# Two graph layers and two attention layers on one core: where the weights of the first attention layer are split, where two stores are waited for, and the order of the q and k blocks

## The reference

```
x = x + (adj @ h) @ W0 + b0
x = x + (norm_adj @ (h @ W1)) + b1               # norm_adj: adj scaled by its rows' degree
x = x + o + layernorm(o)*gamma + beta,  o = attention(h @ w_qkv, masked where adj == 0) @ w_proj + b_proj
x = x + attention(h@Wq+bq, h@Wk+bk, h@Wv+bv, additive mask (1-adj)*-1e9) @ Wo + bo     # 8 heads of 32
```

## Time and profile before

| | |
|---|---|
| median of 3 runs | 2866.49 us (2864.7 to 2868.12) |
| the profiled execution: time, span | 2864.98 us, 2862.8 us |
| span until the graph phase's last matmul | 478.0 us |
| first score matmul of the attention phase | 506.55 us |
| PE busy over the span | 2809.5 us (98%) |
| DVE, ACT, POOL busy | 2319.6, 2175.3, 590.0 us |

### The profile page before, as it was taken

One profiled execution on the slowest core, in us unless ns is written; L12 is line 12 of the kernel. 1 busy time (PEld: TensorE's weight loads), 2 busy tenths in 40 slices (PEclk: granted clock), 3 DMA queues, 4 the chain that ended last, 5 costly groups with the idle time before them and its releaser, 6 DMA issues.

```text
span 2862.8 us, 59796 instructions
## 1 busy us (share of the span) xinstructions
PE 2809.5 (98%) x23872; PEld 2257.2 (79%) x23872; DVE 2319.6 (81%) x4293; ACT 2175.3 (76%) x3926; POOL 590.0 (21%) x538
## 2 busy tenths in 40 slices
PE   7999998999999999999999999999999999999998
PEld 6888887677878787878787878777878777877776
DVE  6866765888888888888888888888888888888876
ACT  3000001889898989898989889898989898989897
POOL 2222221011414141414141415010101010101000
PEclk9999999999999999999999999999999999999999
DMA  3001002323242423333333352323333333323332
GB/s 129 30 30 60 30 30 54 89 60 93 65 100 57 98 66 93 71 92 72 86 78 86 78 144 71 91 66 88 76 86 78 85 79 77 80 70 85 74 75 64
DMA packets 123587, 217.18 MB, mean 76 GB/s; under 512 B 20016, under 2 KB 88240, under 8 KB 123312
## 3 DMA queue, kind: packets, MB, share of 16 engines
q1 hardware_dynamic: 122160, 209.14, 29.4%
q0 software_dynamic: 1152, 4.19, 0.5%
HBM read 53.87 MB, written 25.17 MB: 28 GB/s over the span
## 4 chain that ended last, share of the span: by engine, by line
PE 79%; DVE 2%; ACT 1%; DMA 0%; issue 0%; SPq 0%; ACTq 0%; DVEq 0%
PE t_ring_ps L749 32%; PE t_ot_ps L777 16%; PE t_s_ps L736 16%; PE t_ring_ps L719 4%; PE t_ring_ps L721 4%; PE t_ring_ps L720 4%; PE t_ring_ps L794 1%; DVE t_T L1008 1%; PE t_ring_ps L798 1%; DVE t_PT L1085 1%; PE t_ring_ps L813 0%; DVE t_hT_lo L1020 0%; DMA t_k<-t_st_lo 0%; ACT t_PT L927 0%; ACT t_T L921 0%
## 5 line engine op out<-in xcount | busy, mean ns | idle before, releaser
L1008 DVE CUSTOM_DVE_ANT_0 t_T<-t_s_ps,mask 128x1024 f32<-128x1024 f32 x1024 | 1239.4, 1215 | 55.2 <-PE t_s_ps L736 53.6
L921 ACT ACTIVATE t_T<-t_T,t_low 128x1024 f32<-128x1024 f32 x1024 | 1175.8, 1152 | 59.6 <-DVE t_low L1008 59.5
L749 PEld LDWEIGHTS t_ring_ps<-t_ident,t_T 128*128 128x128 f32 x8192 | 936.5, 141 | 225.0 <-issue 80.3
L749 PE MATMUL t_ring_ps<-t_ident,t_T 128*128 128x128 f32 x8192 | 1102.9, 275 | 9.1 <-DVE t_hT_lo L1020 4.7
L927 ACT ACTIVATE t_PT<-t_ring_ps 128x512 f32<-128x512 f32 x1456 | 812.6, 597 | 114.1 <-PE t_ring_ps L749 93.3
L736 PE MATMUL t_s_ps<-t_k,t_q 128*128 128x512 f32 x2048 | 722.1, 433 | 6.1 <-DMA t_k<-t_st_lo 4.2
L1085 DVE COPY t_PT<-t_ring_ps 128x512 f32<-128x512 f32 x592 | 408.8, 691 | 144.1 <-PE t_ring_ps L749 140.5
L777 PE MATMUL t_ot_ps<-t_PT,shared 128*32 128x256 f32 x8192 | 494.9, 382 | 0.3 <-ACT t_PT L927 0.3
L777 PEld LDWEIGHTS t_ot_ps<-t_PT,shared 128*32 128x32 f32 x8192 | 240.0, 109 | 224.6 <-issue 68.7
L247 ACT ACTIVATE g_yT_hi<-g_ps 128x512 fp32r<-128x512 f32 x64 | 38.3, 598 | 401.3 <-PE g_ps L187 401.3
L736 PEld LDWEIGHTS t_s_ps<-t_k,t_q 128*128 128x128 f32 x2048 | 315.7, 191 | 15.3 <-DMA t_k<-t_st_lo 4.7
(11 more groups left out here) (154 smaller groups left out, 3149.3 us busy)
## 6 DMA issues: line engine op xcount, KB each, us to landing
t_q<-t_st_hi SPq DMA_DIRECT2D x256, 128.0 KB, 2.4
t_k<-t_st_hi SPq DMA_DIRECT2D x256, 128.0 KB, 2.4
t_k<-t_st_lo SPq DMA_DIRECT2D x256, 128.0 KB, 2.5
t_q<-t_st_lo SPq DMA_DIRECT2D x256, 128.0 KB, 2.4
shared<-x_after_graph_layers SPq DMA_DIRECT2D x8, 1024.0 KB, 6.3
t_xe<-x_after_graph_layers SPq DMA_DIRECT2D x32, 256.0 KB, 3.1
x_after_layer<-t_xe SPq DMA_DIRECT2D x32, 256.0 KB, 2.1
shared<-x_after_layer SPq DMA_DIRECT2D x8, 1024.0 KB, 6.6
```

The lines of the kernel that those rows point to most:

```text
L749: last = nc.tensor.transpose(banks[b][:, i * P:(i + 1) * P], T[u % RING][:, kt * P:(kt + 1) * P], ident[:])
L921: nc.scalar.activation(T[u % RING][:], T[u % RING][:], ACT.Exp, bias=low[:, u % RING:u % RING + 1], scale=-1.0, accum_out=rsum[:, u:u + 1] ...
L1008: nc.vector.tensor_tensor_reduce(out=T[u % RING][:], in0=s_ps[u % 2][:], in1=mask[:, qt, :], scale=1.0, scalar=3.4e38, op0=ALU.add, op1=AL ...
```

## The change

Four edits go together:

1. The first attention layer's weights are split inside the graph phase's last job: ACT after its first `yT_hi` of that job, DVE after the normalization of slot 0. To make room, the graph phase's tiles share memory with `PT` and the split weights with `split`; `ident` is made once, for both phases.
2. SP no longer waits for the last two stores and the raw weights at the end of the graph phase. The semaphores `x_left` of these stores are waited for by ACT and DVE before they write `PT`, and by SP before it loads the next x. (The raw weights are waited for by ACT at the split.)
3. q's blocks precede k's in `FIRST`, `MID` and `NEXT`, and `load_head` issues q's four DMAs once q is staged, then k's four once k is.
4. The 13 loads of the second layer move behind the loads of heads 0 and 1, into the tile `o_sb`. Its split moves from before the first mask and exp to the end of the group of units 8 to 11 of the first job, on both ACT and DVE.

```diff
@@ graph_phase, SP, end of the stream
-            for s in range(2, SLOTS):
-                sp.wait_ge(x_stored[s], 16 * ROUNDS)
-            sp.wait_ge(raw_in, 32)
@@ graph_phase, ACT
-            with act.Fori(0, 8 * ROUNDS) as job:
+            with act.Fori(0, 8 * ROUNDS - 1) as job:
                 for g in range(YG):
+                    y_hi(job, g)
+            y_hi(8 * ROUNDS - 1, 0)
+
+            act.wait_ge(raw_in, 32)
+            nc.scalar.activation(next_hi[:, :, 0:D], raw[:, :, 0:D], ACT.Copy, scale=-SCALE).then_inc(next_w_hi, 1)
+            nc.scalar.activation(next_hi[:, :, D:], raw[:, :, D:], ACT.Copy).then_inc(next_w_hi, 1)
+            for g in range(1, YG):
+                y_hi(8 * ROUNDS - 1, g)
@@ graph_phase, DVE, in the last job, after the normalization of slot 0
+                    dve.wait_ge(next_w_hi, 2)
+                    nc.vector.scalar_tensor_tensor(out=next_lo[:, :, 0:D], in0=raw[:, :, 0:D], scalar=-SCALE,
...
+                    nc.vector.tensor_tensor(next_lo[:, :, D:], raw[:, :, D:], next_hi[:, :, D:].bitcast(F32),
+                                            op=ALU.subtract).then_inc(next_w_split, 1)
@@ tables
 FIRST = [("h", 0, 0), ("h", 0, 1), ("h", 1, 0), ("h", 1, 1),
-         ("qk", 0, 0, 0), ("qk", 0, 1, 0), ("qk", 0, 0, 1), ("qk", 0, 1, 1), ("v", 0), ("v", 1), ("v", 2), ("v", 3)]
+         ("qk", 0, 0, 0), ("qk", 0, 0, 1), ("qk", 0, 1, 0), ("qk", 0, 1, 1), ("v", 0), ("v", 1), ("v", 2), ("v", 3)]
@@ attention_phase, SP, load_head
+                for w, to in enumerate((q4, k4)):
+                    if staged is not None:
+
+                        b, n = place[staged[w]]
+                        sp.wait_ge(bank_freed[b], n + 1)
+                    for part in range(4):
...
@@ attention_phase, SP, body, before the load of the next x
+                    if job == 0:
+
+                        for s in range(2):
+                            sp.wait_ge(x_left[s], 32)
@@ attention_phase, PE
-            pe.wait_ge(made, 3)
             for k, what in enumerate(FIRST):
-                if k == 4:
-                    pe.wait_ge(w_split, 1)
@@ attention_phase, ACT
-            weights_hi(0)
             act.wait_ge(bias_zero, 1)
             for n, what in enumerate(FIRST):
                 hi_part(("first", n), what, 0, 0)
-            weights_hi(1)
-            act.wait_ge(bias_done, 1)
             exp(0, 0)
+            for s in range(2):
+                act.wait_ge(x_left[s], 32)
...
+                    if job == 0 and u == NT:
+                        act.wait_ge(bias_done, 1)
+                        weights_hi()
@@ attention_phase, DVE, behind the FIRST blocks and in the body
-            weights_lo(1)
-            dve.wait_ge(bias_done, 1)
             masked(0, 0)
             masked(0, 1)
+            for s in range(2):
+                dve.wait_ge(x_left[s], 32)
...
+                    if job == 0 and u == NT:
+                        dve.wait_ge(bias_done, 1)
+                        weights_lo()
```

More of the change, by code:

```diff
@@ L35, in make_identity, with graph_phase @@
                             pattern=[[-1, P]], channel_multiplier=1).then_inc(made, 1)
-def graph_phase(nc, a, x_mid, mask, shared):
+def graph_phase(nc, a, x_mid, mask, shared, ident, PT, split, x_left):
     B, N, D = a["x"].shape
@@ L93, in graph_phase @@
         x_in = [sem(f"x_in{i}") for i in range(SLOTS)]
-        x_stored = [sem(f"x_stored{i}") for i in range(SLOTS)]
+        x_stored = [sem(f"x_stored{i}") for i in range(2)] + x_left
         at_mm = sem("at_mm")
@@ L123, in graph_phase, with as_weights @@
         AT = 2 * NT
+        def as_weights(rows):
+            return rows[:].rearrange("p t d -> p (t d)").rearrange("p (c o) -> p c o", c=DC)
+        raw, next_hi, next_lo = as_weights(shared[1]), as_weights(split[0]), as_weights(split[1])
         def job_of(m):
@@ L463, in bank_plan, with attention_phase @@
     return place
-def attention_phase(nc, a, x_mid, x_mid2, out, mask, shared):
+def attention_phase(nc, a, x_mid, x_mid2, out, mask, shared, ident, PT, split, x_left):
     B, N, D = a["x"].shape
@@ L486, in pb, with as_weights @@
             return ctx.enter_context(nc.psum_tensor("t_" + name, [P, width], F32))
-        ident = sb("ident", [P, P])
-        w_hi = [sb(f"w_hi{i}", [P, DC, 4 * D], F32R) for i in range(2)]
-        w_lo = [sb(f"w_lo{i}", [P, DC, 4 * D], F32R) for i in range(2)]
+        def as_weights(rows):
+            return rows[:].rearrange("p t d -> p (t d)").rearrange("p (c o) -> p c o", c=DC)
+        w_hi = [as_weights(split[0]), sb("w_hi1", [P, DC, 4 * D], F32R)]
+        w_lo = [as_weights(split[1]), sb("w_lo1", [P, DC, 4 * D], F32R)]
         b_qk = sb("b_qk", [P, 2, 2, 2])
@@ L641, in load_head @@
                     sp.wait_ge(s_done, slot_free)
-                if staged is not None:
-                    b, n = place[staged]
-                    sp.wait_ge(bank_freed[b], n + 1)
-                for part in range(4):
-                    dst = slice(part * HD, (part + 1) * HD)
-                    sp.dma_start(q4[s][dst, :].bitcast(F32), (st_hi, st_lo)[part // 2][0][rows, :].bitcast(F32)).then_inc(head_in[s], 16)
-                    sp.dma_start(k4[s][dst, :].bitcast(F32), (st_hi, st_lo)[part % 2][1][rows, :].bitcast(F32)).then_inc(head_in[s], 16)
+                for w, to in enumerate((q4, k4)):
[3 more added lines that the diff above has]
+                    for part in range(4):
+                        dst = slice(part * HD, (part + 1) * HD)
+                        half = (st_hi, st_lo)[part % 2 if w else part // 2]
+                        sp.dma_start(to[s][dst, :].bitcast(F32), half[w][rows, :].bitcast(F32)).then_inc(head_in[s], 16)
             def load_xe(job, layer, p):
@@ L684, in body @@
                     load_xe(job - 1, before, 3)
-                load_head(job, 4, UNITS * job + 24, key_of(job, ("qk", 1, 1, 1)))
+                load_head(job, 4, UNITS * job + 24, [key_of(job, ("qk", 1, w, 1)) for w in range(2)])
                 if before is not None:
@@ L831, in body @@
                 table = blocks_of(before is None, after is not None)
+                if layer != after and after is not None:
+                    pe.wait_ge(w_split, 1)
                 def block_of(u):
@@ L1275, in build_program @@
         shared = [ctx.enter_context(nc.sbuf_tensor(f"shared{i}", [P, N // P, D], F32)) for i in range(2)]
-        graph_phase(nc, a, x_mid, mask, shared)
-        attention_phase(nc, a, x_mid, x_mid2, out, mask, shared)
+        ident = ctx.enter_context(nc.sbuf_tensor("ident", [P, P], F32))
+        PT = ctx.enter_context(nc.sbuf_tensor("PT", [P, N // P, N // P, P], F32))
+        split = [ctx.enter_context(nc.sbuf_tensor(f"split{i}", [P, N // P, D], F32R)) for i in range(2)]
+        x_left = [ctx.enter_context(nc.semaphore(f"x_left{i}")) for i in range(2)]
+        graph_phase(nc, a, x_mid, mask, shared, ident, PT, split, x_left)
+        attention_phase(nc, a, x_mid, x_mid2, out, mask, shared, ident, PT, split, x_left)
 _INS = ["x", "adj", "L0_gnn_weight", "L0_gnn_bias", "L1_gnn_weight", "L1_gnn_bias", "L2_gnn_w_qkv",
```

107 lines of the change are left out of this document (53 added, 54 removed).

## The result

The changed kernel takes 2859.38 us (median of 8 runs, 2856.44 to 2860.81), the kernel before 2866.35 us (8 runs beside it, 2864.25 to 2868.66). The ratio is 0.9975, its 95% interval 0.9966 to 0.9984: faster by 7.0 us. The forecast was 2857 in a range of 2852 to 2862.

A forecast was written before the change was run, and what follows sets the result against it. TensorE was busy 98% of the span, so time could only be won where it stands still, nearly all between graph and attention phases. Terms summed to 9.4 us, 2855.6 on the profiled execution; forecast 2857, range 2852 to 2862.

The forecast's parts named there:

- store wait: End of graph phase: without SP's wait for the last store, the attention phase starts at 479.8 instead of 483.87, gaining 4.1 us.
- weights split in the graph phase: Start of attention phase: PE starts h at once, qk blocks may start 3.8 us after the phase, not 6.8; gain 3.0.
- clock in the qk blocks: First qk blocks: PE's idle time before them shrinks, so its clock was taken to stay full; gain 1.6 us, ends 0 and 1.7.
- q before k: Head 0's DMAs: q's four go earlier, so k's last lands at 503.99 instead of 506.55; gain 2.6 us.
- second layer's weights leave the start: First mask: it began 1.08 us after the scores and needs some 0.7; gain 0.4 us.
- fill: Filling the attention pipeline, 508.7 to 515.5, where PE ran at half clock: gain 1.5 us if the clock stays up.
- split in job 0 and its clock: Units 8 to 11, first job: the moved split stalls PE, -4.1 us; the clock may fall behind that gap, -0.7.
- switch of layers: Second layer's first job: PE's 1.49 us wait for head 0 shrinks as k's last DMA issues earlier; gain 1.0 us.
- The loads behind the heads: The 13 loads stand before the next x and head 2; biases land at 510, all in time; cost 0.
- only h and the first qk blocks run at half: Rival, chance 0.10: h's transposes are too little work to keep the clock up; gain 6.6 us, time 2860.
- The rival of the clock terms in general: Chance 0.17: the clock falls after the shorter gaps too and behind job 0's stall; gain 4 us, time 2862.5.

The follow-up runs named there:

- the version among the v blocks: Changed kernel with the 13 loads in front again and the second layer's split placed among the first v blocks: 2854.75 us, ratio 0.9962; timed again 2855.02 us.

## Why the prediction was right, and where not

| term | forecast | measured | by |
|---|---|---|---|
| store wait | 4.1 | 4.11 | 4.89 and 0.78 from store to phase |
| weights split in the graph phase | 3.0 | 2.87; undone 2.9 | qk 6.98 earlier, less 4.11 |
| clock in the qk blocks | 1.6 | 0; 1.5 in one profile of three | v at 12.05 or 10.49 |
| q before k | 2.6 | 2.65; undone 2.74 | scores against v |
| second layer's weights leave the start | 0.4 | 0.31 | mask 0.77 behind scores, 1.08 before |
| fill | 1.5 | 2.14 (1.84 by the other profile of before) | 12.04 less 9.90 |
| split in job 0 and its clock | -4.8 | -5.09 | 12.88 less 7.79 |
| switch of layers | 1.0 | 0.81 (0.53 by the other profile of before) | 149.69 less 148.88 |
| sum | 9.4 | 7.8 | |

At job 15 it is 7.29: another 0.5 goes in pieces of under 0.3 over the jobs. The medians are 7.0 apart.

**The mechanisms** stood where the prediction put them. Store wait, split and order of q and k were each undone and gave their price back, the last two in the medians as well (2.0 to 2.3 and 3.2 to 3.5), the store wait on the path alone: 1.2 to 1.5 in the medians; the split in job 0 was taken away in the version among the v blocks and gave 4.7 in the medians, 5.05 in the profile. The loads behind the heads made nobody on the path wait: the biases landed at 513.06, 3 us later than the forecast of 510 on a clock that was by then 2 us behind it, and head 2 was there in time. What their place costs in time is not settled, as the medians with all 13 in front are 1.2 to 1.5 lower.

**The step that failed** is "I take it that the clock stays up: 1.6". PE's idle stretches in front of the qk blocks did shrink to 1.8 and 2.0, and the clock still fell, now 1.4 us into the blocks instead of 0.9. It isn't even a fixed thing: the same program had the full clock in one profile of three. In the profiles where it fell, this is most of the 2.4 by which the median lies above the forecast; the rest is the sum of small ones, the job pieces of 0.5 above all, against the 0.6 that the fill brought more. The rival "only h and the first qk blocks run at half" came half true: the qk blocks did, h didn't. That its 2860 lies nearer the measured 2859.4 than the forecast is luck, since it takes 1.2 off for h, which ran at full. The rival of the clock terms in general had it right only in its gap behind the stall: the fill ran at the full clock and brought more than its term, 2.14.

**The rule weighed against the trace.** By the Trainium skill ("TensorE: Matmul & The Clock Gate", "Part 4: PE-mode transpose") transposes don't count as activity for the clock. In the run with the store wait put back PE did nothing but transposes from 483.01 on, at half clock, and the clock was back at full before the first qk matmul at 488.01. This speaks against the rule as the earlier trace rows does: there, and in the second profile of the kernel before, the clock also came back while PE had run transposes alone. That the clock fell behind the transposes of the changed kernel would fit it, but the same transposes with the same gaps left it up in the second profile. What decides between these is open.

**What was in no term of the sum** is the fall of the clock at the end, 2.5 us in two of the changed kernel's three profiles. The change alone doesn't bring it: the third profile has none. Whether the change makes it more frequent is open: nine of the 12 profiles with the change or parts of it show it, neither of the two of the kernel before does, and both of these are at that kernel's best mean clock of 0.996. Its slower runs, at 0.994 and below, were not profiled.

## What to carry to other kernels

A split, a copy or a cast that must be moved out of a startup goes where its own engine has only slack work left, not merely out of the way: the same four instructions cost 5.1 us in a full pipeline (a fall of the clock included), 2.4 with the second engine's half one group later, where it needn't wait for the first, and 0.1 between the last staged block and the first score. When a group of DMAs gates a start, issue those whose data is ready first. Look at what else is in flight then: in one profile 13 loads ahead made the last DMA land 1.1 us later, though that version was no slower by its median. And price a clock that is to "stay up" as a coin toss unless several profiles of the same program agree.
